# Router logits from a stationary gate in four column groups of TensorE

## The reference, cut to what matters

```
x = x + autocorrelation(layernorm(x), ctx, ctx)   # 8 heads; correlation over lags by FFT, the 8 best
                                                  # lags of each channel, softmax, weighted sum of lags
h = layernorm(x)                                  # 2048 tokens x 512
logits = h @ gate_w.T                             # 16 experts
probs  = softmax(logits); the 2 best, rescaled to sum 1
x = x + sum over chosen experts of w * (silu(g) * u) @ w_down   # g, u = split(h @ w_gate_up), 128 wide
      + (silu(gs) * us) @ shared_down                           # shared expert, 512 wide
```

## Time and profile before

| | |
|---|---|
| median of 3 runs | 509.39 us (508.45 to 509.79) |
| the profiled execution | 509.03 us, of it the span 507.2 us |
| TensorE clock granted in the span | 0.996 of 2.4 GHz |
| attention loop and its end | 0 to about 203 us |
| routing | about 203 to 245 us |
| experts and shared expert | about 245 us to the end |

### The profile page before, as it was taken

One profiled execution on the slowest core, in us unless ns is written; L12 is line 12 of the kernel. 1 busy time (PEld: TensorE's weight loads), 2 busy tenths in 40 slices (PEclk: granted clock), 3 DMA queues, 4 the chain that ended last, 5 costly groups with the idle time before them and its releaser, 6 DMA issues.

```text
span 507.2 us, 8574 instructions
## 1 busy us (share of the span) xinstructions
PE 476.8 (94%) x2097; PEld 328.1 (65%) x2098; DVE 312.2 (62%) x972; ACT 222.7 (44%) x425; POOL 227.3 (45%) x384
## 2 busy tenths in 40 slices
PE   4789999999999999898899999999999999999997
PEld 2556556656655655356576667766667678888885
DVE  3799899999999863884133333333333566747643
ACT  4778888888888835200122222122221435022120
POOL 2356676676667544044333333333333026466520
PEclk9899999999999999999999999999999999999999
DMA  4416533424253031801435555455554314555622
GB/s 157 163 43 237 173 110 127 145 63 146 68 180 114 36 103 43 331 0 43 124 113 157 165 165 151 150 158 161 165 153 151 131 63 126 159 174 165 207 62 83
DMA packets 24923, 66.76 MB, mean 132 GB/s; under 512 B 3456, under 2 KB 3456, under 8 KB 23488
## 3 DMA queue, kind: packets, MB, share of 16 engines
q1 hardware_dynamic: 18576, 45.74, 25.0%
q0 software_dynamic: 6320, 20.71, 15.6%
HBM read 45.73 MB, written 20.71 MB: 131 GB/s over the span
## 4 chain that ended last, share of the span: by engine, by line
PE 62%; DVE 15%; POOL 8%; issue 8%; ACT 5%; DMA 1%; SPq 0%; DVEq 0%; POOLq 0%; ACTq 0%
PE bank L457 19%; PE bank L655 17%; PE bank L670 8%; PE bank L643 4%; DVE top_v L923 4%; POOL arena L1198 4%; PE bank L469 4%; POOL arena L1201 4%; PE bank L558 2%; DVE arena L928 2%; PE bank L567 2%; DVE stats L886 2%; DVE resid L911 2%; ACT arena L772 2%; ACT arena L771 2%
## 5 line engine op out<-in xcount | busy, mean ns | idle before, releaser
L655 PEld LDWEIGHTS bank<-wgu_sb,x2T 128*128 128x128 f32 x376 | 67.6, 189 | 41.0 <-issue 33.6
L655 PE MATMUL bank<-wgu_sb,x2T 128*128 x376 | 92.0, 388 | 2.1 <-ACT x2T L814 0.6
L814 ACT COPY x2T<-bank 128x512 f32<-128x512 f32 x47 | 27.5, 585 | 142.6 <-PE bank L643 142.6
L1251 POOL DMA_INDIRECT xg_sb<-x_rows,gidx x47 | 45.9, 976 | 98.0 <-PE bank L643 93.6
L1083 DVE COPY actT_both<-bank 128x128 f32<-128x128 f32 x47 | 13.7, 291 | 73.3 <-PE bank L664 73.3
L670 PE MATMUL bank<-arena,actT_both 128*128 x94 | 47.9, 593 | 0.0
L457 PE MATMUL bank<-act_lo 128*128 128x512 f32 x96 | 41.2, 538 | 6.7 <-DVE act_lo L965 6.7
L457 PE MATMUL bank<-tokens_hi,shgu_hi 128*128 128x512 f32 x92 | 36.2, 394 | 0.0
L457 PE MATMUL bank<-tokens_hi,shgu_lo 128*128 128x512 f32 x92 | 35.8, 389 | 0.0
L457 PE MATMUL bank<-tokens_lo,shgu_hi 128*128 128x512 f32 x92 | 35.8, 389 | 0.0
L457 PEld LDWEIGHTS bank<-act_lo 128*128 128x128 f32 x96 | 18.7, 197 | 22.8 <-issue 20.8
(11 more groups left out here) (153 smaller groups left out, 1077.7 us busy)
## 6 DMA issues: line engine op xcount, KB each, us to landing
y_rows<-x2T SPq DMA_DIRECT2D x47, 256.0 KB, 3.1
wgu_sb<-w_gu SPq DMA_DIRECT2D x8, 1024.0 KB, 5.3
resid<-x SPq DMA_DIRECT2D x16, 256.0 KB, 2.8
arena<-ctx SPq DMA_DIRECT2D x16, 256.0 KB, 3.3
x_rows<-arena SPq DMA_DIRECT2D x16, 256.0 KB, 2.1
result<-resid SPq DMA_DIRECT2D x16, 256.0 KB
arena<-w_down SPq DMA_DIRECT2D x1, 3072.0 KB, 13.0
shgu_sb<-sh_gu SPq DMA_DIRECT2D x1, 2048.0 KB, 8.0
```

What stands on the lines that cost most here:

```text
L655: last = mm(ps_gu[b][:, 0:2 * INTER], xgT[b][:, c * P:(c + 1) * P], wgu_sb[:, bass.ds(at + c * 2 * INTER, 2 * INTER)], start=c == 0, stop= ...
L814: copy(xgT[b], ps_xgT[:, :]).then_inc(xgT_ready, 1)
L1251: nc.gpsimd.indirect_dma_start(xg[b], None, x2_rows[:, :], bass.IndirectOffsetOnAxis(ap=gidx[b][:, 0:1], axis=0)).then_inc(gathered[b], 16)
```

## The change

The operands of the gate product change places. The gate block (128 features x 32 columns, 16 of them experts and 16 zeros) is now stationary, and the transposed tile (128 tokens) moves. Block c's product goes to the 32 partitions from 32c on, that is to its own column group of the array. The four partial results are not added in PSUM, they lie side by side: 128 partitions (4 blocks x 32) by 128 tokens. ACT copies this square out (`by_chunk`). A second, small product, with the square stationary and a constant of four stacked 32x16 identities (`chunk_sum`) moving, adds the four blocks and turns the result to tokens x experts. ACT copies that into `logits`.

Where things stand: the first product is at L502's place. The small product comes behind the even spectrum (L514) and waits for ACT's copy of the square. That copy is at L757's place in ACT's stream; the logits copy stands behind L772 and in front of L723. For pairs 0 to 13 both products use the bank of the output, `ps_out`: the first waits for the residual add of pair n-2 (for pairs up to 13, in n up to 16), and `output(p)` waits for the logits of pair p-3. For pairs 14 and 15 they use the even bank. PE's wait for the logits copy in front of L514 goes away. In iteration 17 the small product comes behind two pieces of shared work, eight matmul instructions.

```diff
+GW = 32
...
+    ("chunk_sum", E), ("identity", P), ...
+        "chunk_sum": np.tile(np.eye(GW, E), (KB, 1)), ...
-        gate_sb = sb("gate_sb", [P, KB * E])
+        gate_sb = sb("gate_sb", [P, KB * GW])
+        by_chunk = sb("by_chunk", [P, P])
...
+        def ps_chunks(p):
+
+            return ps_out if p < PAIRS - 2 else ps_w_even
...
             def output(p):
                 wait(pe, resid_ready, p)
+                wait(pe, logits_ready, p - 2)
...
                 if live(n, -3):
                     p, pb = pair(h, b, -3)
                     pe.wait_ge(x2T_ready, p + 1)
+                    if n <= PAIRS:
+                        wait(pe, resid_ready, p + 2)
+                    else:
+                        pe.wait_ge(out_products_ready, 2 * PAIRS - 1)
+                        wait(pe, logits_ready, p if n > PAIRS + 1 else 0)
                     for c in range(KB):
-                        last = mm(ps_w_even[:, 0:E], x2T_tile[pb][:, c * P:(c + 1) * P], gate_sb[:, c * E:(c + 1) * E],
-                                  start=c == 0, stop=c == KB - 1)
-                    last.then_inc(logits_psum, 1)
+                        last = mm(ps_chunks(p)[c * GW:(c + 1) * GW, 0:P], gate_sb[:, c * GW:(c + 1) * GW],
+                                  x2T_tile[pb][:, c * P:(c + 1) * P], start=True, stop=True)
+                    last.then_inc(chunks_psum, 1)
                 if n == PAIRS + 1:
                     shared_half(0, 0, 1, range(2, KB))
                     pe.wait_ge(resid_ready, PAIRS)
+                    pe.wait_ge(logits_ready, PAIRS - 2)
                     shared_half(0, 1, 0, range(2))
                 if live(n, -1):
                     p, _ = pair(h, b, -1)
                     pe.wait_ge(lagwT_ready, p + 1)
                     mm(ps_w_odd[:, :], C["odd"], lagwT, start=True, stop=True).then_inc(w_odd_psum, 1)
-                    wait(pe, logits_ready, p - 1)
                     mm(ps_w_even[:, :], C["even"], lagwT, start=True, stop=True).then_inc(w_even_psum, 1)
+                if live(n, -3):
+                    p, pb = pair(h, b, -3)
+                    pe.wait_ge(chunks_ready, p + 1)
+                    mm(ps_chunks(p)[:, P:P + E], by_chunk[:, :], C["chunk_sum"], start=True, stop=True).then_inc(logits_psum, 1)
...
                 if live(n, -3):
                     p, _ = pair(h, b, -3)
-                    act.wait_ge(logits_psum, p + 1)
-                    copy(logits[:, bass.ds(p * E, E)], ps_w_even[:, 0:E]).then_inc(logits_ready, 1)
+                    act.wait_ge(chunks_psum, p + 1)
+                    wait(act, logits_psum, p)
+                    copy(by_chunk[:, :], ps_chunks(p)[:, 0:P]).then_inc(chunks_ready, 1)
...
                     nc.scalar.mul(w_odd_sw[64:128, :], ps_w_odd[0:64, :], -1.0).then_inc(w_odd_sw_ready, 1)
+                if live(n, -3):
+                    p, pb = pair(h, b, -3)
+                    act.wait_ge(logits_psum, p + 1)
+                    copy(logits[:, bass.ds(p * E, E)], ps_chunks(p)[:, P:P + E]).then_inc(logits_ready, 1)
...
-        "gate": blocks(L0_ffn_gate_w),
+        "gate": blocks(np.concatenate([np.asarray(L0_ffn_gate_w), np.zeros((GW - E, D), np.float32)])),
```

More of the change, by code:

```diff
@@ L119 @@
     ("out_even_plain", P), ("out_even_swapped", P), ("out_odd", P),
-    ("identity", P), ("earlier", P), ("ones", P), ("count", P), ("tile_edge", E),
+    ("chunk_sum", E), ("identity", P), ("earlier", P), ("ones", P), ("count", P), ("tile_edge", E),
     ("token", PAIRS),
@@ L133, in constants @@
         "out_odd": inverse_spectrum(1, 0.5),
-        "identity": np.eye(P), "earlier": np.triu(np.ones((P, P)), 1), "ones": np.ones((P, P)),
+        "chunk_sum": np.tile(np.eye(GW, E), (KB, 1)), "identity": np.eye(P), "earlier": np.triu(np.ones((P, P)), 1), "ones": np.ones((P, P)),
         "count": np.tile(p, (P, 1)), "tile_edge": np.tile(P * np.arange(E), (P, 1)),
@@ L321, in build @@
         logits_psum, logits_ready = sem("logits_psum"), sem("logits_ready")
+        chunks_psum, chunks_ready = sem("chunks_psum"), sem("chunks_ready")
         route_step, route_diff, route_exp = sem("route_step"), sem("route_diff"), sem("route_exp")
```

## The result

In twenty runs each, the changed kernel took 512.03 us (510.15 to 513.71) and the kernel before 510.44 (508.37 to 512.31): a ratio of 1.0031, 95% interval 1.0017 to 1.0045, or 1.6 us more (0.9 to 2.3). The profiled execution took 510.85 us, its span 509.1, against 509.03 and 507.2 before. Slower, as forecast, and 512.03 is inside the range of 511.0 to 515.2; but the kernel is slower by less than half of the 3.8 us of the sum.

The account below looks back on a forecast made before the run. The prediction took a cycle of DVE, POOL and PE to bound the loop, with the gate off it. Terms 0.2 + 0.2 + 1.2 + 1.5 + 0.7 = 3.8 us gave 512.8 us, by the median 513.2; range 511.0 to 515.2.

Parts of the forecast that it names:

- The rival that PE paces the loop: Attention loop: a shorter gate saves 0.43 us in each of twelve iterations, 5.2 us, giving 505.7 us; chance 0.06.
- The one that the loop slips: Attention loop: DVE's chain takes the 0.20 us whole, or PE a drain more; 2.4 us over twelve iterations, 515.2; chance 0.16.
- Step 1: Iterations 3 to 14: added copies and product almost wholly hidden, 0.02 us an iteration, 0.2 us in all.
- Step 2: Iteration 15: the logits copy in front of ACT's normalisation, itself directly before PE's transposes, is in the open; 0.2 us.
- The gate's length: Gate product on PE: eight slots of 0.107 us, 0.86 us in all, against 0.81 for the old gate.
- step 4: Iteration 17: logits copy waits for the small product behind eight shared matmuls, delaying normalisation and last transposes; 1.5 us.
- each crossing: Moving to or from the column groups may let the array run empty, adding 0.16 us each time; gate up to 1.2.
- The rival of full overlap: Column groups overlap fully, gate 0.21 us, three gates give back 1.9 us, 510.9; chance 0.22, shared with partial overlap.
- its own signs: Forecast wrong if loop period moves over 0.05 us, gate takes under 0.5, or first routing maximum's shift is missing at end.
- Step 3: Iteration 16: gate waits 0.94 us for DVE's residual add, is 0.05 longer, small product adds 0.22; 1.2 us.
- Step 5: Iteration 18: chunk copy and small product come between the gate and the logits copy; 0.7 us.
- Passed on: From the first routing maximum to the end: no gap covers the delay, so the whole 3.8 us reaches the end.

Follow-up runs that it names:

- one_group: Changed kernel with all four gate blocks accumulating in one column group, copy and small product cut to 32 rows; 514.51 us, ratio 1.007.
- one_group_wide: Changed kernel with all four gate blocks in one column group, copy and small product kept at 128 rows; 513.13 us, ratio 1.0051.
- old_last: Changed kernel with another bank from pair 13, iteration 17's logits copy behind the normalisation, iteration 18's logits in the old form; 509.7 us, ratio 0.9977; again 509.89, 0.9987.
- copy_behind: Changed kernel with ACT's logits copy moved behind the last pair's normalisation, in iteration 17 only; 511.04 us, ratio 1.0014.

## Why the prediction came out as it did

*What bounds the loop.* Right. The forecast that a gate product off the cycle of DVE, POOL and PE could neither gain nor lose held in every kernel, with gate slots of 0.36 and of 0.97 us. The rival that PE paces the loop (0.06) is refuted by PE's wait for ACT growing by what the gate saved. (Its price was off too: against the old gate's 0.81 its own terms give 0.81 - 0.21 - 0.22 = 0.38 us an iteration, 4.6 in twelve, not 5.2.) The one that the loop slips (0.16) did not happen either, but it was near on PE's side. In front of L477 only 0.02 to 0.06 us of idle time are left. In one_group, with its small product of 0.41 us, there are none in most iterations, and L477 starts 0.12 to 0.15 us behind POOL's result in place of 0.05; the loop column was still 155.68.

*Step 1, 0.2 us: 0.* Step 2, iteration 15, 0.2 us: nothing to be seen, the loop column holds it and stands 0.02 us under before. Both steps charged the logits copy with its duration of 0.18. Its cost in ACT's queue is less: L740 starts 0.69 us after L790 (103.31 to 104.00), where before it was 0.61 from L772 to L723 (103.79 to 104.40), so 0.08. The Trainium skill (ScalarE: Activation LUTs, What ACT_TABLE_LOAD costs) says that ACTIVATEs back to back overlap by about 93 ns. The trace agrees for a copy with an ACTIVATE behind it: the copy takes 0.17 us and the ACTIVATE starts 0.07 to 0.09 us after it.

*The gate's length* is the term that was mis-sized. I took 0.86 us of slots by the rows of full-width matmuls and gave the overlap a chance of 0.22. Measured: 0.36, with another 0.10 in front of it (196.08 - 195.12 - 0.86), so 0.46 against 0.86. Three times on the path, that is 1.2 us of the 1.9 by which the sum was too high. What I had against the overlap, that the two passes of a block stand next to each other in one quarter, did not hold: the matmuls start in two sets of four. one_group and one_group_wide show that it is the overlap: 1.85 us of tail for taking it away. The other 0.7 us are 0.4 of steps 1 and 2, 0.2 of ACT's stall in step 4, and the small product.

The Trainium skill (TensorE: Matmul & The Clock Gate, Part 3) says that three column tiles gave 2.38 times; here four gave 0.99 / 0.35 = 2.8. The Trainium skill (TensorEngine Tiling (Array Packing), Key Properties) says that a change of tiling mode drains TensorE. The 0.10 us in front of the gate fit that, and are less than the 0.16 that I allowed for each crossing. They could as well be its first weight load, which starts only at 196.07 and not ahead of its slot, as that of the old gate did (195.30 for 195.73); no run tells the two apart.

*Where the numbers agree by luck.* The rival of full overlap had 1.9 us less than the sum, and 1.9 us less is what the tail shows; but it had all of it from a gate of 0.21 us, where the gate gave 1.2. The span's 1.9 us (507.2 to 509.1) is a sum as well: 0.5 less at the start, 1.9 more in the tail, 0.9 more in the routing, 0.5 less behind it. And the range was laid around 509.39 us, the median of three runs of the kernel before, while that of twenty is 510.44. On the old figure the measured 1.6 us would have given 511.0, the lower end of the range.

*By its own signs* the forecast was wrong where it named a gate under 0.5 us as such a sign; the period did not move, and the shift at the first routing maximum, 1.9 us of tail, was passed on. Of the signs in the loop, L918's wait for L749 did not double (0.15 to 0.16 us) and the residual add's idle time did not go (2.0 us as before), both since the logits copy costs ACT 0.08 us. The cover of 0.36 us that I gave the gate is 0.41 by its own figures (101.70 less 101.29).

*Step 3, iteration 16, 1.2 us: 0.74*, from output to output (8.27 against 7.53). The wait for the residual add is there as forecast: the gate starts 2.00 us after L477, where it was 0.97 after L469, so 1.03, with the crossing, in place of 0.94. The shorter gate takes 0.45 off it, the small product puts 0.14 on (I had 0.22). Together that is 0.72. Taking the wait away is worth 0.74, not 1.03, since the normalisation chain is next.

*Step 4, iteration 17, 1.5 us: 0.92*, from output to transposes (6.13 against 5.21). The order in ACT's queue is the cause as forecast: moving one copy behind the normalisation gives back exactly 0.92. The stall behind the shared matmuls is 1.28 us (199.97 to 201.25) where I summed 1.46; the gate had gained 0.35 before it.

*Step 5, iteration 18, 0.7 us: 0.25*, from transposes to the first maximum (2.96 against 2.71). The chunk copy and the small product cost what they should (the gate's last result at 203.13, logits copy at 203.95: 0.82, where it was 0.04), the gate itself is 0.62 us shorter to its last result (0.42 against 1.04), and it starts 0.10 later. In old_last it is 0 again.

*Passed on.* Right: routing and rest hold no gap. In the changed profile the routing is 0.9 us longer, and the next section tells why. The rest averages 261.62 us in the nine profiles with the new gate and 262.02 in the three of before; that would account for timed differences that lie under the tail's. The two ranges touch, no run was made to tell why, and it stays open.

## What to carry to other kernels

A shorter product pays only where its end is what somebody waits for; in the loop here the engine that was 94% busy simply waited longer. When a step is split into two with a copy between, place each half in every queue that it passes and look at the last iterations by themselves: of the 1.91 us that this change cost, 1.66 were one bank that was still being read and one 16-column copy in front of a normalisation, and came back with another bank and a moved copy. The other 0.25 us were the second copy and product of the last pair, with nothing beside them. And before judging a tail by how much was taken off one engine, look for the chain that runs beside it and ends at the same time.

## What the runs showed of the hardware that I had not expected

Four column groups overlap, even with two fp32 passes each: eight matmuls of 128 columns, 0.27 to 0.30 us each to their result, are all done 0.43 us after the first starts, against 1.03 to 1.06 in one group. The two sets start 0.13 us apart, but the next line's first matmul only 0.20 us after the last of them, so the eight take 0.36 us of slots.

A small product of 32 rows between products of 128 rows cost 0.41 us, one of 128 rows 0.14 (one_group against the changed kernel). Fewer rows were dearer.

TensorE's granted clock fell once in the routing of the changed kernel's profile. Busy time of PE in a stretch: length, busy us and instructions, clock, DMA share, GB/s.
```profile
239.00:240.00 1.00, 0.96 (x8) 1.00 0.00 0
240.00:241.00 1.00, 0.77 (x4) 0.55 0.00 0
241.00:242.00 1.00, 1.00 (x6) 0.50 0.00 0
242.00:243.00 1.00, 1.00 (x4) 0.50 0.00 0
243.00:244.00 1.00, 1.00 (x3) 0.74 0.00 0
```
That is 1.2 in place of 2.4 GHz for some 3 us, after PE had been idle for 1.19 us and 0.28 us between short products (of 96 columns); eight of these took 1.99 us where they took 1.10 before, and this is the 0.9 us by which the routing column stands out. The kernel before has idle times of 1.20 and 0.28 us in the same place and kept its clock there in three profiles; of the nine with the new gate, two lost it (copy_behind's fell beside a wait and cost 0.2). The timed runs have one clock for the whole span. In the profiles it is 0.996 or 0.997, but 0.990 to 0.993 in the five with this loss or with the longer one at the start. Of the timed runs of the kernel before beside the experiments, 11 of 29, 14 of 29 and 8 of 23 have 0.993 or less, so it too loses the clock in some executions; of the changed kernel's twenty 15 have. Whether the change makes it more frequent, and so has a part in the 1.6 us, was not tested.
